# A graph-convolution kernel: 86 of 1592 row gathers replaced by column copies out of a feature table held in SBUF

## The chip, the cores and the metric

One Trainium2 chip, one core. The time is device time of that core in microseconds (us), from start to end of one execution; lower is better. Engines are named as in the profile: PE (TensorE), PEld (its weight loads), DVE (VectorE), ACT (ScalarE), POOL (GpSimd), SP (SyncE, which here only issues DMAs). A "q" behind an engine's name means its sequencer: instructions that are handled before the engine itself, such as register loads or DMA issues.

## The reference, cut to what matters

Two message-passing layers over a graph of 6250 nodes and 206,250 edges sorted by destination, 128 features. The change lies in the second:

```
edge_index = jnp.stack([src, dst])
...
h = jnp.maximum(_layernorm(x, axis=-1), 0.0)
...
filters = jax.nn.silu(edge_attr @ fW1 + fb1) @ fW2 + fb2
messages = (x[src] @ dW + db) * filters
aggregated = jax.ops.segment_sum(messages, dst, num_segments=x.shape[0])
upd = jax.nn.silu(aggregated @ uW1 + ub1) @ uW2 + ub2
return x + upd
```

Here `x[src]` is the normalised row `h` of each edge's source. The kernel computes `h @ dW + db` once per node, so an edge needs one row of a table of 6250 rows.

## The kernel before, in words

Edges are cut into **units** of 768: 6 chunks of 128 edges, one edge to a partition. 269 units make 45 **turns** of 6 units (the last has 5); the unit's place in its turn is its slot s. Because edges are sorted by destination, each unit adds into a window of 32 destination columns.

The program has three parts one after another: `prepare` (about 90 us: first layer norm, tables, windows), `attention_edges` (about 2000 us) and `convolution_edges` (about 2000 us). Attention gathers rows of 132 floats from table0; while it runs it finishes nodes in tiles of 128: normalises them, turns the tile with PE (features onto partitions), multiplies by dW, adds db and has SP store the rows to table1 in DRAM (L799) and the skip rows to `sent` (L800). The last seven tiles are done after the loop and stored at L814.

Convolution, for every unit n:

- **POOL** (`gather_units`, L688) issues one indirect DMA for each chunk (L63), which fetches 128 rows of 128 floats from table1 into `xg[:, s, c]`. It waits only for indices and for the slot to be free, that is for the message of the unit six before (L697, `xg_free` is `s_msg`). Each slot has its own arrival semaphore; `landed_by` (L556) gives its count. In every second turn one chunk of slot 4 is left out by POOL.
- **SP** (`load_indices`, L620; `Carry.collect`, L608) fetches that chunk in POOL's place with 128 DMAs of one row each, over two turns. It reads 16 row addresses at a time into registers (L613), issues 16 DMAs (L617), and copies the chunk into xg when the slot is free (L642).
- **ACT** computes SiLU of the hidden layer (L1387) and issues the loads of edge attributes (L1370).
- **PE** computes in iteration n the hidden layer of unit n (L1441), the filters of unit n-1 (L1417, needs the SiLU of n-1 and the message of n-3), and the sum over edges of unit n-3 (L1426). It also updates finished tiles (L1438, L1415).
- **DVE** adds in iteration n the sum of unit n-4 to the window (`merge`, L1504), makes the one-hot matrix of unit n-1 (L1484), adds the bias to its filters (L1490), waits for the gathered rows and multiplies (L1496). At the head of each turn it loads six window starts into registers (`bases`, L500).

The loops of DVE, ACT and PE have one turn as their body, written out unit by unit; POOL and SP have two and four. The addresses of gathered rows, windows and one-hot keys are registers; every instruction with such an address has a register instruction before it. `sums` is three planes of 6304 columns in SBUF: during convolution, plane 0 holds the sums and plane 1 the skip rows; plane 2 is free.

Of the kernel before, what the change touches and what calls it, by code (L numbers as in the profile page):

```python
# [24 lines left out]
P = 128  # L25
CH = 6
UE = CH * P
SL = 6
# [87 lines left out]
def prepare(nc, h, a, acc, state, typ, table, project, sources):  # L116


    with ExitStack() as ctx:
# [15 lines left out]
        dev, inv, shift, eps, early = sb("dev", [P, G]), sb("inv", [P, G]), sb("shift", [P, G]), sb("eps", [P, 1]), sb("early", [P, 1])  # L135
        ps_e, ps_x, ps_s, ps_l, ps_t = pb("ps_e"), pb("ps_x"), pb("ps_s", 512), pb("ps_l", 1024), pb("ps_t", 512)
# [17 lines left out]
        def _(sp):  # L154
# [28 lines left out]
            sp.dma_start(row_starts(state), a["src_rows"][:, :]).then_inc(lists_in, 16)  # L183
            project.load_rows(sp, a)
            for g in range(GROUPS - 1):
# [9 lines left out]
                if g:  # L195
                    store(g - 1)
            store(GROUPS - 2)
# [9 lines left out]
            sp.wait_ge(out_done[1], 16 * GROUPS)  # L207

        @block.gpsimd
        def _(pool):  # L210
# [44 lines left out]
            pool.wait_ge(lists_in, 16)  # L255
# [241 lines left out]

def bases(nc, engine, h, first, count):
# [40 lines left out]

LOAD = 3  # L540
# [15 lines left out]
def landed_by(pace, r, i, s, carried=0, j=0):  # L556

    if s != CARRY_SLOT:
# [61 lines left out]
def load_indices(nc, sp, a, h, idx, idx_in, gathered, landed, carry, xg, xg_free, ahead=lambda r, i, v: None, beside=lambda r, i: None,  # L620
                 behind=lambda r, i: None, listed=lambda: None):
# [22 lines left out]
    def span(r, t, b, first=False):  # L644

        for q in range(span_turns * LOADS):
# [4 lines left out]
            if q == 0 and first:  # L651
                listed()
# [35 lines left out]
def gather_units(pool, passes, table, xg, width, idx, idx_in, gathered, xg_free, pool_turn, carry):  # L688
    span_turns, carried_chunks = carry.pace.span, carry.pace.carried

    with pool.Fori(0, passes) as r:
        def turn(i, first, count, carried=None):
            for s in range(count):
# [5 lines left out]
                taken = carried is not None and s == CARRY_SLOT  # L699
# [21 lines left out]
def attention_edges(nc, h, a, acc, state, typ, table, messages, sent, y, project, sources, following):  # L721

    with ExitStack() as ctx:
# [23 lines left out]
        landed, pool_turn, steps, key_ready, begun, rise_zero = (  # L747
            sem(k) for k in "landed pool_turn steps key_ready begun rise_zero".split())
# [32 lines left out]
        def _(sp):  # L781
# [21 lines left out]
            sp.sem_inc(stored, 32)  # L803
            load_indices(nc, sp, a, h, idx, idx_in, gathered, landed, carry, xg, s_sum, beside=beside, behind=behind)
# [4 lines left out]
            sp.wait_ge(stored, 32 * (passes * DONE + 1))  # L809
            first_indices(sp, a, following.idx, following.idx_in)  # L810
            for n, k in enumerate((1, 0)):
                a0, a1 = HALVES[k]
                sp.wait_ge(t_hdc, n + 1)
                sp.dma_start(messages[(LAST + a0) * P:(LAST + a1) * P, :].rearrange("(t p) r -> p t r", p=P), l_hd[:, a0:a1, :]).then_inc(last_stored, 16)  # L814
            sp.wait_ge(last_stored, 32)

        @block.gpsimd
        def _(pool):
            gather_units(pool, project.pool_passes, table, xg, ROW, idx, idx_in, gathered, s_sum, pool_turn, carry)
# [18 lines left out]
        def _(act):  # L838
            nc.scalar.copy(acc[:, 1:NT, 0:NP], acc[:, 0, 0:NP].unsqueeze(1).to_broadcast([P, NT - 1, NP]))
            with act.Fori(0, pass_count(act, h)) as r:  # L840
# [55 lines left out]
                def relus(k):  # L896

                    act.wait_ge(stored, 32 * k)
# [162 lines left out]
        def _(dve):  # L1061
# [9 lines left out]
            with dve.Fori(0, pass_count(dve, h)) as r:  # L1071
                def tile(i, s):
# [4 lines left out]
                    if closes(i) and s == 1:  # L1077
                        dve.wait_ge(stored, 32 * (r * DONE + i - OPEN))
                        nc.vector.tensor_copy(p.turned, ps_c[:, P:2 * P])
                        nc.vector.tensor_tensor(p.relu, p.rows, p.relu, ALU.add)  # L1080
                    if closes(i) and s == 2:
                        nc.vector.tensor_tensor(p.turned, ps_c[:, 2 * P:3 * P], p.db, ALU.add)
# [180 lines left out]
class Project:  # L1263


    def __init__(self, nc, ctx):
        sb = lambda name, shape: ctx.enter_context(nc.sbuf_tensor("pj_" + name, shape, fp32))
        self.w, self.dw, self.bias = sb("w", [P, NT, D]), sb("dw", [P, D]), sb("bias", [P, NT, D])
        parts = sb("parts", [P, 3, D])
        self.relu, self.turned, self.db = (parts[:, k, :] for k in range(3))  # L1270
# [4 lines left out]
        self.carry_turn = ctx.enter_context(nc.semaphore("pj_carry_turn"))  # L1275
        self.raise_from = self.tile[:, :, 0:TILES]
# [23 lines left out]
def convolution_edges(nc, h, a, acc, update, table, sent, sources, project, y, out):  # L1300

    with ExitStack() as ctx:  # L1302
# [17 lines left out]
        sem_landed = sem("landed")  # L1320
# [304 lines left out]
```

## Time and profile before

| | us |
|---|---|
| median of 3 runs | 4103.61 (4102.91 to 4105.91) |
| span of the profiled execution (first to last instruction) | 4098.5 |
| mean granted TensorE clock in that execution | 0.60 |
| POOL busy | 3050.9 (74%) |
| PE busy | 3358.1 (82%) |
| DVE busy | 2405.1 (59%) |
| ACT busy | 1368.9 (33%) |

The runs give a time alone; the profile gives one further execution's span. Around its span lie launch and end, which no row divides. Busy shares are averages over three parts with different loads: DVE's, for example, is far higher in attention than in convolution. A matmul's end is modelled, and a POOL gather's busy time leaves out the sequencer's part between two of them.

### The profile page before, as it was taken

Reading aid. Unit: us, or ns where it says so; the run is one execution under the profiler, and the core shown is the slowest. Engines: PE = TensorE matmul, PEld = TensorE weight load, DVE = VectorE, ACT = ScalarE, POOL = GpSimd, SP = SyncE. Lnnn points to the kernel's source line nnn. Section 1 sums busy time; section 2 is a strip of 40 time slices with the busy share of each in tenths; the row PEclk is TensorE's granted clock in tenths of the full one; section 3 lists DMA queues with packets and bytes.
Section 4 is the critical chain, followed back from the end, with each engine's and each line's share of the span. In section 5 each row is a group of like instructions: output and inputs, shape, how many; then the busy total and the mean of one; then the engine's idle time right before and its main releaser. Section 6 shows DMA issues by size and latency. Waiting matters only on the chain. (4 is left out here: it accounts for less than half of the span.)

```text
span 4098.5 us, 63699 instructions
## 1 busy us (share of the span) xinstructions
PE 3358.1 (82%) x14005; PEld 2625.3 (64%) x14006; DVE 2405.1 (59%) x5327; ACT 1368.9 (33%) x3398; POOL 3050.9 (74%) x3216
## 2 busy tenths in 40 slices
PE   5788888888888888888768898888888888888798
PEld 3566666666666666666656676766766666666676
DVE  7888888888888888888853333333333332333333
ACT  5455555555555555555421111111111111111111
POOL 6777777777777777777757777777777777777776
PEclk7555555555555555555567666667666677667767
DMA  4222222222222222222232222222222222222222
GB/s 125 58 60 61 61 60 61 62 60 61 61 60 61 61 61 60 61 61 59 59 88 78 79 74 78 79 74 78 75 77 78 75 78 78 74 79 74 78 78 62
DMA packets 190049, 288.10 MB, mean 70 GB/s; under 512 B 85904, under 2 KB 132811, under 8 KB 185384
## 3 DMA queue, kind: packets, MB, share of 16 engines
q0 software_dynamic: 101888, 212.13, 20.6%
q1 hardware_dynamic: 83160, 33.99, 3.5%
q10 hardware_dynamic: 4840, 40.55, 3.2%
q14 instruction: 147, 1.20, 0.1%
q8 instruction: 14, 0.23, 0.0%
HBM read 271.07 MB, written 12.49 MB: 69 GB/s over the span
## 5 line engine op out<-in xcount | busy, mean ns | idle before, releaser
L63 POOL DMA_INDIRECT ce_xg<-table,ce_idx x1592 | 1509.2, 948 | 491.6 <-issue 481.5
L63 POOL DMA_INDIRECT ae_xg<-table,ae_idx x1592 | 1502.5, 944 | 491.2 <-issue 489.6
L1496 DVE TENSOR_TENSOR ce_msg<-ce_ring,ce_xg 128x768 f32<-128x768 f32 x269 | 257.6, 958 | 1151.0 <-DMA ce_xg<-table,ce_idx 1150.6
L948 PE MATMUL ae_ps_k<-ae_xg,ae_e 128*96 128x129 f32 x3224 | 882.7, 432 | 0.0
L1417 PEld LDWEIGHTS ce_ring<-ce_fw,ce_hid 128*128 128x128 f32 x3228 | 586.6, 278 | 435.6 <-DVE ce_msg L1496 314.6
L1417 PE MATMUL ce_ring<-ce_fw,ce_hid 128*128 128x128 f32 x3228 | 649.6, 377 | 262.1 <-DVE ce_msg L1496 261.8
L948 PEld LDWEIGHTS ae_ps_k<-ae_xg,ae_e 128*96 128x96 f32 x3224 | 689.6, 277 | 126.7 <-issue 117.2
L1387 ACT ACTIVATE ce_hid<-ce_ps_h,ce_fb 128x768 f32<-128x768 f32 x269 | 241.8, 899 | 1235.4 <-PE ce_ps_h L1441 692.2
L1441 PE MATMUL ce_ps_h<-ce_ea,ce_fw 50*128 50x384 f32 x1076 | 548.3, 641 | 19.0 <-DMA ce_ea<-in_edge_attr 17.1
L1426 PEld LDWEIGHTS ce_ring<-ce_hot,ce_msg 128*128 128x128 f32 x3224 | 528.4, 253 | 3.0 <-DVE ce_msg L1496 2.9
L1426 PE MATMUL ce_ring<-ce_hot,ce_msg 128*128 128x32 f32 x3224 | 514.3, 319 | 1.0 <-DVE sums L1504 1.0
L868 ACT ACTIVATE ae_off<-cst,plan 128x96 bf16<-128x96 f32 x1614 | 454.1, 363 | 5.0 <-DVE plan L491 5.0
L860 ACT ACTIVATE ae_upper<-ring 128x576 f32<-128x576 f32 x269 | 174.9, 650 | 668.3 <-DVE ring L1125 668.3
L996 PE MATMUL ring<-ae_rise,cst 64*128 64x192 f32 x538 | 270.4, 605 | 84.2 <-DVE ae_rise L1148 81.2
L963 PE MATMUL ae_ps_tz<-cst,ae_high 128*96 128x128 f32 x269 | 120.7, 449 | 251.8 <-DVE ae_high L1135 251.8
L1441 PEld LDWEIGHTS ce_ps_h<-ce_ea,ce_fw 50*128 50x128 f32 x1076 | 227.2, 234 | 145.1 <-issue 65.8
L1135 DVE TENSOR_REDUCE ae_high<-ae_e 128x96 f32<-128x576 f32 x269 | 304.8, 1133 | 0.0
L1490 DVE TENSOR_TENSOR ce_ring<-ce_ring,ce_fb 128x768 f32<-128x768 f32 x269 | 258.3, 960 | 71.5 <-PE ce_ring L1417 71.2
L1125 DVE TENSOR_TENSOR ring<-ring,ae_xg 128x576 f32<-128x576 f32 x269 | 206.1, 766 | 126.0 <-DMA ae_xg<-table,ae_idx 122.3
L963 PEld LDWEIGHTS ae_ps_tz<-cst,ae_high 128*96 128x96 f32 x269 | 41.9, 156 | 316.6 <-DVE ae_high L1135 316.6
L996 PEld LDWEIGHTS ring<-ae_rise,cst 64*128 64x128 f32 x538 | 134.0, 308 | 171.4 <-DVE ae_rise L1148 158.2
L844 ACT ACTIVATE ae_e<-ae_e 128x576 f32<-128x576 f32 x269 | 183.7, 683 | 105.6 <-DVE ae_e L1157 105.5
(186 smaller groups left out, 3336.2 us busy)
## 6 DMA issues: line engine op xcount, KB each, us to landing
ae_stage<-table SPq DMA_DIRECT2D x2560, 0.5 KB
ce_stage<-table SPq DMA_DIRECT2D x2560, 0.5 KB
ce_ea<-in_edge_attr ACTq DMA_DIRECT2D x88, 450.0 KB
ae_xg<-table,ae_idx POOLq DMA_INDIRECT x1592, 2.5
ce_xg<-table,ce_idx POOLq DMA_INDIRECT x1592
sums<-in_x SPq DMA_DIRECT2D x7, 448.0 KB, 4.6
table<-sums SPq DMA_DIRECT2D x6, 462.0 KB, 3.5
pj_bias<-in_x_rows SPq DMA_DIRECT2D x42, 64.0 KB
```

The source lines that it names most:

```text
L63: eng.indirect_dma_start(out=out, out_offset=None, in_=table[:, :], in_offset=bass.IndirectOffsetOnAxis(ap=idx, axis=0)).then_inc(done, 16)
L868: last = nc.scalar.activation(off[:, s % 2, c, :], h.iota, ACT.Square, bias=keys[:, c:c + 1], scale=STEP)
L948: last = nc.tensor.matmul(ps_k[0:KEYS, 0:D + 1], by_chunk[s % 3][:, c, :], xg[:, s % XS, c, 0:D + 1], start=(c == 0), stop=(c == count - 1))
L996: nc.tensor.matmul(ps_m[s % 2][:, 0:2 * KEYS], h.raised_by[0:64, :], rise[:, :, :].rearrange("p a k -> p (a k)"), start=True, stop=True).t ...
L1125: nc.vector.tensor_tensor(by_kind, by_kind, xg[:, s % XS, :, D + 1:ROW].unsqueeze(3).to_broadcast([P, CH, NT, W]), ALU.add).then_inc(s_ful ...
L1135: nc.vector.tensor_reduce(out=high[:, :], in_=by_chunk[s % 3].rearrange("p c k -> p k c"), op=ALU.max, axis=AX.X).then_inc(s_high, 1)
L1387: nc.scalar.activation(hid[:, b, :].rearrange("p (k e) -> p k e", k=2), ps_h[:, :].rearrange("p (k e) -> p k e", k=2)[:, :, 0:H], ACT.Silu ...
L1417: last = nc.tensor.matmul(ps_f[b][:, c * D:(c + 1) * D], hid[:, b, c * P:(c + 1) * P], fw2[:, :], start=True, stop=True)
L1426: last = nc.tensor.matmul(ps_a[s % 2][:, 0:W], msg[:, s % 3, c, :], hot[:, s % 3, c, :], start=(c == 0), stop=(c == count - 1))
L1441: last = nc.tensor.matmul(ps_h[:, k * 512:k * 512 + H], fw1[:, :], ea[:, s // LOAD, q:q + H], start=True, stop=True)
L1490: nc.vector.tensor_tensor(filt, filt, fb2[:, :].unsqueeze(1).to_broadcast([P, CH, D]), ALU.add).then_inc(s_bias, 1)
L1496: nc.vector.tensor_tensor(msg[:, s % 3, :, :], filt, xg[:, s % XS, :, :], ALU.mult).then_inc(s_msg, 1)
```

## The change

In each of the turns 2 to 44 (43 turns), the last chunk of slots 1 and 3 is no longer gathered by POOL. In its place:

- Attention stores the turned tile too, so that DRAM holds `features` [128 features][6272 nodes]: one more store by SP in each of 42 tiles and one for the last seven. The projected rows get a buffer of their own (`p.message`), so that the turned ones last until stored.
- `prepare` converts the 86 lists of 128 source nodes from 4-byte to 2-byte numbers on POOL and writes them to DRAM; convolution loads them into partition 0.
- Early in convolution SP loads all of `features` (128 partitions x 25,088 bytes) into plane 2 of `sums`.
- In turns 1 to 43, for two columns of work m = 0, 1 in slots 0-2 and 3-5: DVE copies nodes 0-63 and ACT nodes 64-127 of the list, each copy one column [128 x 1] from the table into `held`, at an address from a register. Registers are loaded eight at a time from 2-byte numbers. Batches are 24, 24 and 16 copies. ACT does this behind the unit's SiLU, DVE between the bias and the wait for the gathered rows.
- PE multiplies `held` by dW into 128 spare columns of a filter bank, ahead of the filters; DVE adds db and writes the chunk into xg (`place`). The chunk for slot 1 of the next turn is placed at slot 5, that for slot 3 at slot 2 of the next turn.
- Two semaphores become common to both layers (`pool_turn`, `carry_turn`), which changes no order.

```
+COLUMNS = (Column((0, 1, 2), 5, 1), Column((3, 4, 5), 2, 3))
+COLUMN_TURNS = TURNS - 2
+BATCHES = ((0, 24), (24, 48), (48, 64))
+ENGINE_SHARE = P // 2
+FETCH = 8
...
+def sources_at(nc, engine, columns, i, m, first):
+    return nc.values_load_multi_w_load_instructions(columns[:, bass.ds(((i - 1) * len(COLUMNS) + m) * P + first, FETCH)], engines=[engine],
...
-                taken = carried is not None and s == CARRY_SLOT
+                taken = carried is not None and s == CARRY_SLOT or s in to and not (isinstance(i, int) and i < 2)
                 for c in range(CH - 1 if taken else chunks_of(i, s)):
...
# attention_edges, SP, closes(i)
-                    sp.dma_start(messages[bass.ds((i - OPEN - 1) * P, P), :], p.turned).then_inc(stored, 16)
+                    sp.dma_start(messages[bass.ds((i - OPEN - 1) * P, P), :], p.message).then_inc(stored, 16)
+                    sp.dma_start(features[:, bass.ds((i - OPEN - 1) * P, P)], p.turned).then_inc(stored, 16)
...
# convolution_edges, SP, once, behind the first index load
+            def tables(r):
+                sp.wait_ge(scaled, 1)
+                sp.wait_ge(project.last_turned, 16)
+                sp.wait_ge(s_column, r * COLUMN_TURNS * len(COLUMNS) + len(COLUMNS))
+                sp.dma_start(by_node, features[:, :]).then_inc(table_in, 16)
...
# convolution_edges, ACT, behind the SiLU of slot s (DVE's is the same with columns e and tensor_copy, s_half)
+                def collect(i, s):
+                    m = s // 3
+                    e0, e1 = BATCHES[s % 3]
+                    if s % 3 == 0:
+                        act.wait_ge(s_column, column_at(r, i, m) + 1)
+                        act.sem_inc(begun, 1)
+                    if s == 0:
+                        act.wait_ge(table_in, 16 * (r + 2))
+                        act.sem_inc(begun, 1)
+                    for e in range(e0, e1, FETCH):
+                        nodes = sources_at(nc, mybir.EngineType.Activation, columns, i, m, ENGINE_SHARE + e)
+                        for k, node in enumerate(nodes, ENGINE_SHARE + e):
+                            last = nc.scalar.copy(held[:, m, k:k + 1], by_node[:, bass.ds(node, 1)])
+                    if s % 3 == 2:
+                        last.then_inc(s_other, 1)
...
# convolution_edges, PE, ahead of the filters of slot b
+                def products(i, m, b):
+                    k = column_at(r, i, m)
+                    pe.wait_ge(s_half, k + 1)
+                    pe.wait_ge(s_other, k + 1)
+                    nc.tensor.matmul(ps_x[b], held[:, m, :], project.dw[:, :], start=True, stop=True).then_inc(s_column, 1)
...
# convolution_edges, DVE
+                def place(i, m, b):
+                    column = COLUMNS[m]
+                    dve.wait_ge(s_column, column_at(r, i, m) + 1 + len(COLUMNS))
+                    dve.wait_ge(s_msg, r * UNITS + i * SL + column.to + 1 + XS)
+                    nc.vector.tensor_tensor(xg[:, column.to, CH - 1, :], ps_x[b], project.db, ALU.add).then_inc(s_placed, 1)
...
+                    aside(r, at)     # place, then collect
                     dve.wait_ge(s_bias, n)
                     carry.landed(dve, r, s, carried)
+                    for m, to in enumerate(TO):
+                        if s == to and not (isinstance(i, int) and i < 2):
+                            dve.wait_ge(s_placed, column_at(r, i - 1, m) + 2)
```

## Rows read from the trace of the kernel before

**Rows 1.** The chain that ended last, from the page:
```profile
POOL 35%; issue 12%; DMA 1%; POOLq 1%; DVE 0%; PE 0%; ACT 0%; DVEq 0%
```

**Rows 2.** Groups by line over the span: xcount | busy us, mean ns | idle us before
```profile
L63 POOL DMA_INDIRECT ce_xg<-table,ce_idx x1592 | 1509.2, 948 | 491.6 <-issue 481.5
L63 POOL DMA_INDIRECT ae_xg<-table,ae_idx x1592 | 1502.5, 944 | 491.2 <-issue 489.6
```

**Rows 3.** Gathers of POOL in order of time, the first and the last: start us, us
```profile
2091.94 0.98 POOL L63 DMA_INDIRECT ce_xg<-table,ce_idx  x1 [6.47 <-DVEq L1473]
...
4085.35 0.94 POOL L63 DMA_INDIRECT ce_xg<-table,ce_idx  x1 [0.30 <-issue]
```

**Rows 4.** Who waited for whom, 2200 to 4000 us: us in total, times, longest
```profile
DVE ce_msg L1496 <- DMA ce_xg<-table,ce_idx: 1057.0, 242, 10.3
...
POOL ce_xg L63 <- DVE ce_msg L1496: 3.3, 11, 0.3
```

**Rows 5.** Busy us of each engine in a stretch about one turn long
```profile
core 0: us, PE busy (x) PEld busy (x) DVE busy (x) ACT busy (x) POOL busy (x), PEclk, DMA share, GB/s
...
2545.00:2590.00 45.00, 34.36 (x178) 27.98 (x177) 14.07 (x27) 5.66 (x7) 34.03 (x37) 0.73 0.28 76
```

**Rows 6.** DVE: two one-column instructions in order of time; L1146, ns min/median/max
```profile
47.00 0.15 DVE L438 TENSOR_SCALAR narrow<-wide 128x1 f32<-128x1 f32 x1
47.07 0.14 DVE L439 TENSOR_SCALAR passes<-wide 128x1 int32<-128x1 f32 x1
...
L1146 DVEq FUSED_REGOPS  x269: 57/57/71, 84.4 to 2058.2; - x135
L1146 DVE COPY ae_rise<-state x269: 240/241/243, 85.2 to 2058.5; 1x96 f32 x135
```

**Rows 7.** ACT: one column, ns; six of L868 in order of time; L868, ns
```profile
L894 ACT ACTIVATE pj_few<-pj_few x42: 202/203/203, 202.8 to 2021.9; 128x1 f32<-128x1 f32 x42
...
2017.27 1.69 ACT L868 ACTIVATE ae_off<-cst,plan 128x96 bf16<-128x96 f32 x6
...
L868 ACT ACTIVATE ae_off<-cst,plan x1614: 358/362/374, 77.4 to 2041.0; 128x96 bf16<-128x96 f32 x180
L868 ACTq FUSED_REGOPS  x1476: 46/46/60, 205.1 to 2017.3; - x185
```

**Rows 8.** Register loads, ns: attention's eight values, convolution's six twice, SP's sixteen, one
```profile
L500 DVEq TENSOR_LOAD <-base_i x45: 752/1845/1868, 112.0 to 2055.9; - x45
...
L500 DVEq TENSOR_LOAD <-base_i x1: 1412/1412/1412, 3023.7 to 3023.7; - x1
...
L500 DVEq TENSOR_LOAD <-base_i x1: 805/805/805, 3068.4 to 3068.4; - x1
...
L613 SPq TENSOR_LOAD <-ce_lists x160: 1132/1208/1696, 2126.1 to 3881.8; - x160
...
L113 ACTq TENSOR_LOAD <-passes x2: 295/948/1600, 60.5 to 2097.4; - x2
```

**Rows 9.** SP's sequencer at its loop's end: last branch and what came next
```profile
L666 SPq COMPARE_BRANCH  x1: 61/61/61, 2467.6 to 2467.6; - x1
L666 SPq FUSED_REGOPS  x1: 154/154/154, 2470.4 to 2470.4; - x1
```

**Rows 10.** Two stretches of 10 us at either clock, columns as in rows 5
```profile
2142.00:2152.00 10.00, 8.37 (x56) 6.58 (x55) 2.20 (x4) 2.63 (x3) 7.56 (x9) 0.99 0.78 191
...
2182.00:2192.00 10.00, 10.00 (x33) 7.44 (x32) 2.29 (x4) 1.16 (x2) 7.55 (x9) 0.50 0.20 54
```

**Rows 11.** SP's issues in order of time: a tile's store, and three loads of 448 KB
```profile
2052.49 0.43 SPq L800 DMA_DIRECT2D sent<-pj_parts  x1
...
2124.39 1.68 SPq L1354 DMA_DIRECT2D sums<-sent  x3
```

**Rows 12.** DVE and POOL at convolution's start, in order of time
```profile
2092.42 5.31 DVE L1475 MEMSET sums<- 128x6304 f32 x1 [1.29 <-issue]
...
2095.73 4.15 POOL L63 DMA_INDIRECT ce_xg<-table,ce_idx  x1 [0.30 <-issue]
```

More of the change, by code:

```diff
@@ L537, in __init__, with collects, places, column_chunks @@
         self.chunks = (span * SL * np.arange(1, carried + 1) + CARRY_SLOT) * CH + CH - 1
+class Column:
+    def __init__(self, collected, placed, to):
+        self.collected, self.placed, self.to = collected, placed, to
+        self.late = placed < collected[-1]
+COLUMNS = (Column((0, 1, 2), 5, 1), Column((3, 4, 5), 2, 3))
+COLUMN_TURNS = TURNS - 2
+TO = [column.to for column in COLUMNS]
+BATCHES = ((0, 24), (24, 48), (48, 64))
+ENGINE_SHARE = P // 2
+FETCH = 8
+STORES = 48
+def collects(i):
+    return not (isinstance(i, int) and not 1 <= i <= COLUMN_TURNS)
+def places(i, column):
+    first = 2 if column.late else 1
+    return not (isinstance(i, int) and not first <= i < first + COLUMN_TURNS)
+def column_chunks():
+    turn = np.arange(2, TURNS)
+    return np.stack([(turn * SL + to) * CH + CH - 1 for to in TO], 1).reshape(-1)
+def column_at(r, i, m):
+    return r * COLUMN_TURNS * len(COLUMNS) + (i - 1) * len(COLUMNS) + m
 LOAD = 3
@@ L718, with attention_edges @@
 assert XS == SL
-def attention_edges(nc, h, a, acc, state, typ, table, messages, sent, y, project, sources, following):
+def attention_edges(nc, h, a, acc, state, typ, table, messages, features, sent, y, project, sources, following):
     with ExitStack() as ctx:
@@ L1268, in __init__ @@
         self.w, self.dw, self.bias = sb("w", [P, NT, D]), sb("dw", [P, D]), sb("bias", [P, NT, D])
-        parts = sb("parts", [P, 3, D])
-        self.relu, self.turned, self.db = (parts[:, k, :] for k in range(3))
+        parts = sb("parts", [P, 4, D])
+        self.relu, self.turned, self.db, self.message = (parts[:, k, :] for k in range(4))
         self.rows, self.x = (self.bias[:, k, :] for k in (1, 2))
@@ L1297, with convolution_edges @@
 UPDATE_SLOT = 3
-def convolution_edges(nc, h, a, acc, update, table, sent, sources, project, y, out):
+def convolution_edges(nc, h, a, acc, update, table, features, listed, by_node, sent, sources, project, y, out):
     with ExitStack() as ctx:
@@ L1415, in filters @@
                         nc.tensor.matmul(tile_y, one_hid[:, :], update.w2[:, :], start=True, stop=True).then_inc(t_v, 1)
+                    for m, column in enumerate(COLUMNS):
+                        if at is not None and at[1] == column.placed and places(at[0], column):
+                            products(at[0] - 1 if column.late else at[0], m, b)
                     for c in range(CH):
@@ L1443, in turn @@
                         if not (first and s < 1):
-                            filters(n - 1, (s - 1) % SL, first and s < 3, i if s else None)
+                            filters(n - 1, (s - 1) % SL, first and s < 3, i if s else None, (i, s))
                         if not (first and s < 3):
@@ L1485, in one_hot, with collect, aside, messages @@
                                             keys.unsqueeze(2).to_broadcast([P, CH, W]), ALU.is_equal)
-                def messages(n, s, i, carried, j=0):
+                def collect(i, s):
+                    m = s // 3
+                    e0, e1 = BATCHES[s % 3]
+                    if s % 3 == 0:
+                        dve.wait_ge(s_column, column_at(r, i, m) + 1)
+                        dve.sem_inc(begun, 1)
+                    if s == 0:
+                        dve.wait_ge(table_in, 16 * (r + 2))
+                        dve.sem_inc(begun, 1)
+                    for e in range(e0, e1, FETCH):
+                        nodes = sources_at(nc, mybir.EngineType.DVE, columns, i, m, e)
+                        for k, node in enumerate(nodes, e):
+                            last = nc.vector.tensor_copy(held[:, m, k:k + 1], by_node[:, bass.ds(node, 1)])
+                    if s % 3 == 2:
+                        last.then_inc(s_half, 1)
+                def place(i, m, b):
[3 more added lines that the diff above has]
+                    nc.vector.tensor_tensor(xg[:, column.to, CH - 1, :], ps_x[b], project.db, ALU.add).then_inc(s_placed, 1)
+                def aside(r, at):
+                    if at is None:
+                        return
+                    i, s = at
+                    for m, column in enumerate(COLUMNS):
+                        if s == column.placed and places(i, column):
+                            place(i - 1 if column.late else i, m, (s - 1) % SL % 2)
+                    if collects(i):
+                        collect(i, s)
+                def messages(n, s, i, carried, j=0, at=None):
                     filt = ps_f[s % 2][:, 0:CH * D].rearrange("p (c f) -> p c f", c=CH)
```

79 lines of the change are left out of this document (52 added, 27 removed).

## The prediction

> **What bounds the kernel now.** I read the chain of waits first: it names POOL and its issue, and nothing else above 1% [rows 1]. The groups by line say with what: 1592 gathers in convolution, 0.948 us busy each, and 0.3 us of issue between two [rows 2]. From the first to the last of them pass 1993.4 us [rows 3], 1.25 us a gather. Does POOL wait for anyone? The table of waits says no: in 1800 us it waited 3.3 us for DVE's messages, and nearly all its idle time is its own issue [rows 2]. The engine behind it, DVE, waits 1057 us for gathered rows [rows 4]. So convolution is 1592 x 1.25 us of POOL's work, with a short tail, and removing a gather removes 1.25 us, as long as what takes its place fits beside it. Attention is bound in the same way and keeps all its gathers.
>
> A turn has 36 chunks, less one in every second turn: 44.3 us. In it DVE is busy 14.1 us and ACT 5.7 us [rows 5]. The change spends that idle time.
>
> **What goes.** 2 x 43 = 86 gathers x 1.25 us = 107.5 us. A turn of POOL falls from 44.3 to 41.8 us. That is the most there is to gain.
>
> **What comes on DVE, per turn.** 128 copies of one column. Two static one-column instructions start 0.07 us apart though each lasts 0.15 us [rows 6]; an address from a register adds a register instruction of 0.057 us ahead [rows 6]. Sum 0.13 us, so 16.6 us. The bounds are 0.07 us (register step hidden) and 0.24 us (as long as the 96-column copy, no overlap [rows 6]): 9 to 31 us. I take 0.13, the sum of the rows nearest in shape.
>
> 16 register loads. No row loads 2-byte numbers. Nearest rows [rows 8]: eight 4-byte values 1.85 us; six 1.41 us in one turn and 0.81 us in the next; sixteen 1.13 to 1.21 us; one value 0.30 us at best. One account fits all: a value read alone costs about 0.24 us, and a 16-byte piece that starts on a multiple of 16 bytes costs about the same as a value. The six start at byte 24i - 16: a multiple of 16 only in even turns, where they are one piece and two values (3 x 0.27); else six (6 x 0.235). The eight start at 24i - 12, never a multiple: 8 x 0.23. The sixteen are four pieces: 4 x 0.28. The new lists hold eight 2-byte numbers, 16 bytes, on a multiple of 16. If the piece is counted in bytes, a load is one read, 0.3 to 0.5 us; if 2-byte numbers are read one by one, it is 1.85 us. I take 0.4 us (6.4 us a turn), because four reads are saved in every row where alignment allows it; the other end is the main rival.
>
> Here a page of the Trainium skill speaks against the change: "Runtime: NRT & Kernel Launch", Instruction fetch mechanics, gives about 200 ns for each register loaded, even in bulk. By it the loads would be 16 x 8 x 0.2 = 25.6 us a turn on each engine. By that rule, eight values at 1.85 us agree and sixteen at 1.21 us (0.075 each) do not [rows 8].
>
> The loop's body grows from some 60 to over 300 instructions. SP's body is of that size, and behind its last branch 2.8 us pass before the next instruction [rows 9]. I charge DVE and ACT 2.8 us a turn; bounds 0 and twice that, if two blocks are fetched.
>
> Two placements per turn: 0.3 us each, somewhat over the 96-column copy [rows 6]. DVE's sum: 14.1 + 16.6 + 6.4 + 1.1 (window starts, mean of the two in rows 8) + 0.6 + 2.8 = 41.6 us if nothing overlaps, against POOL's 41.8. But most of the loads overlap: the sequencer reads registers while the engine works off the 2.3 us (a sixth of 14.1 [rows 5]) of message, merge, one-hot and bias that each unit queues ahead. Up to 2 us a unit are hidden this way, so about 35 us. It fits, with 7 us to spare.
>
> **On ACT**: six L868 take 1.69 us at 0.362 us each, so they start 0.265 us apart, overlapping by 0.10 [rows 7]. A one-column instruction of 0.203 us [rows 7] then starts every 0.105 us; with its register step of 0.046 us 0.12, at most 0.25 us. 128 x 0.12 = 15.4 us, loads 6.4, own work 5.7, branch 2.8: 30 us of 41.8. Behind the collect of a unit (24 x 0.12 + 3 x 0.4 = 4.1 us) waits ACT's next SiLU, and PE waits for that. PE's iteration is 28 matmul records: at the low clock (granted 0.50, 1.2 GHz) 33 run in 10 us, so 8.5 us; at the high one (0.99, 2.4 GHz) 56 in 8.4 us, so 4.2 us [rows 10]. SiLU (0.9 us, a sixth of 5.66 [rows 5]) + 4.1 us fit inside 8.5 but not inside 4.2, so PE catches up at 5 to 5.5 us a unit in place of 4.2. POOL now asks for a unit every 7.0 us. Two products a turn add 2 of 28 records twice, 1.2 us at the low clock. PE works at either clock by turns; it still catches up.
>
> **Ring.** DVE's wait on a product or on the table holds the merges and messages queued behind it, and POOL's gather waits for the message of six units before: 6 x 7.0 less landing, some 35 us of slack. POOL waits at 3.3 us in 1800 today, so this slack is nearly unused [rows 4].
>
> **Opening.** SP issues the 3.2 MB table behind three loads of 448 KB at about 2126 us [rows 11]. DMA moved 191 GB/s in a stretch with such a load against 54 GB/s without [rows 10], so some 140 GB/s are free: 4.5 MB land by about 2158. DVE and ACT want it near 2143 (36 gathers after 2092, the 3 us that one of them lost [rows 12], landing), so they stand some 15 us, covered by the 35. Cost 0; bound 10 us. The next four `sent` loads and 128 staged rows queue behind the table on SP's ring; they are due at turn 2, after 2180.
>
> **Small parts, SP's queue.** 42 more stores by SP at 0.43 us [rows 11], one of last tiles, one list store and two list loads: SP's attention stores lie where POOL waits for nobody; at the change of stages about 1 us shows. `prepare` adds a small POOL conversion. Together 2 us, bounds 0 and 6.
>
> **Sum.** The profiled execution spans 4098.5 us, 5.1 below the median of 4103.6, which holds launch and end too. 4098.5 - 107.5 + 4 (2 of small parts, 2 of waits by bunching) = 3995 span; by the median 4000 us. This case's own range is 3993 to 4022.
>
> **Rivals.**
> *A, DVE is full (slower).* Place: the register loads in DVE's `collect`. At 1.85 us each, 16 are 29.6 us; 35.2 + 29.6 less 12 hidden (2 us in each of six units) is 53 us a turn, against 44.3 before: 43 x 8.7 = +374, 4478 us. The point from which it decides: full gain up to 1.15 us a load, nothing left from 1.3 us. For it: eight values do cost 1.85 today, and no row has 2-byte numbers. Against: aligned rows are cheap. ACT would be full at the same time.
> *B, part of the gain.* Loads near 1.2 us, copies near 0.2 us, or PE late at the low clock: 4022 to 4095 us.
> *C, copies hold POOL off.* 3.8 DVE copies fall on each gather. A gather beside a DVE memset took 4.15 us [rows 12]. If each copy kept POOL off for 0.1 us, a gather would come every 1.63 us and a turn take 33.5 x 1.63 = 54.6 us, 4547 in all; at 0.03 us, 45.7 us, 4164. Against: gathers in attention, beside 96-column copies, are as short (0.944 us) as in convolution [rows 2, 6]. For this rule see "SBUF — State Buffer", Who interferes with whom: an fp32 copy in a two-port mode locks GpSimd out of a shared port. [...]
> *D, PE.* Waits for late SiLUs break up its work, the granted clock stays at 0.50, and 8.5 us plus 0.2 us of products a unit exceed POOL's 7.4 of before: 52 us a turn, 4440; half of that if only at times. Against: ACT's 5 us fit inside the low clock's 8.5.
> *E, it does nothing.* The gathers left out could be hidden anyway; rows 4 exclude that.
>
> **Chances.** Forecast 0.62; B 0.10; a result within 0.2% (8 us; about what a measurement of this kernel can tell from no change) 0.03; A 0.16; C 0.05; D 0.04. Faster: 0.72; slower 0.25. The overall range is 3993 to 4280: it takes in B and the milder half of C and D.
>
> **What would show it.** Right: 1506 gathers in convolution, still 0.95 us each and 1.25 apart; POOL's wait for L1496's successor still a few us; new DVE and ACT copy groups of 5504, starting 0.13 and 0.12 us apart; register loads of 0.3 to 0.5 us; DVE still waiting for gathered rows in most units. Wrong: loads over 1.2 us, POOL waiting for messages, DVE's waits for DMA gone (A); gathers longer than 1 us (C); granted clock near 0.5 with PE busy all through convolution (D).

## The result, and the profile after

| | before | after |
|---|---|---|
| median of 4 runs, us | 4104.76 (4102.91 to 4105.97) | 4761.07 (4757.27 to 4763.82) |
| span of the profiled execution | 4098.5 | 4760.1 |
| mean granted TensorE clock | 0.60 | 0.56 |

The change costs 656 us: ratio 1.160, 95% interval 1.158 to 1.161. The forecast was 4000 us, the range 3993 to 4280. What happened is rival A, DVE full by its register loads, and its price of 4478 was itself some 280 us short. DVE's turn, from branch to branch of its loop, takes 60.5 us on average; POOL's was 44.4 before.

The chain of the kernel after, by engine and by line, stands against [rows 1], where POOL held 35%:

```profile
DVEq 25%; DVE 16%; issue 13%; PE 1%; DMA 1%; POOL 0%; SPq 0%; ACT 0%; POOLq 0%
DVEq L506 22%; DVE ce_held L1599 10%; DVE ce_ring L1624 3%; DVE ce_hot L1583 1%; DVEq L512 1%; DVEq L1599 1%; DMA sums<-features 0%; DVE ce_msg L1634 0%; DVE sums L1642 0%; POOL ce_xg L63 0%; DVE ce_xg L1608 0%; DVEq L1583 0%; DVEq L1642 0%
```

POOL is gone from the chain. A quarter of the span is DVE's sequencer (DVEq), and nearly all of that is one line: L506, the register loads of the node lists, 22%. Second come the copies (L1599).

Next the groups by line: count, busy us and mean ns, idle before. They answer to [rows 2].

```profile
L63 POOL DMA_INDIRECT ce_xg<-table,ce_idx x1506 | 1425.1, 946 | 1214.2 <-DVE ce_msg L1634 793.9
L63 POOL DMA_INDIRECT ae_xg<-table,ae_idx x1592 | 1502.9, 944 | 491.2 <-issue 487.5
L1599 DVE COPY ce_held<-sums 128x1 f32 x5504 | 716.1, 154 | 1080.0 <-issue 1079.6
L1473 ACT COPY ce_held<-sums 128x1 f32 x5504 | 624.2, 191 | 1058.9 <-issue 1058.4
```

The 86 gathers are gone, and those left are as short as before (0.946 us), also beside 5504 DVE copies. But POOL, which waited 3.3 us for DVE's messages in 1800 [rows 4], now waits 794 us for them. The group of the copies shows where DVE's time is: it stood idle 1080 us ahead of them with the label "issue": it waited for nothing that the profile shows, and its own sequencer was at work.

The table of waits between 2300 and 4600 us (us in total, times, longest) has no line for DVE waiting for gathered rows, which led it before with 1057 us [rows 4]:

```profile
DVE ce_held L1599 <- issue: 964.5, 720, 2.3
ACT ce_held L1473 <- issue: 926.2, 611, 1.8
POOL ce_xg L63 <- DVE ce_msg L1634: 747.9, 191, 8.8
...
PE ce_ring L1508 <- DVE ce_msg L1634: 249.2, 90, 5.8
```

So the order of who waits for whom has turned round: PE and POOL wait for DVE, DVE and ACT mostly for their own sequencers. The line that had to be bounded blind, register loads of 2-byte numbers (ns min/median/max):

```profile
L506 ACTq TENSOR_LOAD <-ce_columns x688: 1707/1723/1964, 2149.2 to 4704.1; - x172
L506 DVEq TENSOR_LOAD <-ce_columns x688: 1822/1826/1937, 2149.2 to 4715.2; - x172
```

Eight 2-byte numbers take DVE 1.83 us, 0.228 us each, though all of them lie in one aligned 16-byte piece. That is the dear end of the bound (1.85), to 0.02 us.

What one such load does is to be seen in DVE's timeline (start, us, what, idle before):

```profile
3000.76 0.96 DVE L1634 TENSOR_TENSOR ce_msg<-ce_ring,ce_xg 128x768 f32<-128x768 f32 x1
3001.64 0.18 DVE L1642 TENSOR_TENSOR sums<-sums,ce_ring 128x32 f32 x1
3001.73 0.35 DVE L1583 TENSOR_TENSOR ce_hot<-cst,key 128x192 f32<-128x192 f32 x1
3002.00 0.95 DVE L1624 TENSOR_TENSOR ce_ring<-ce_ring,ce_fb 128x768 f32<-128x768 f32 x1
3003.53 1.04 DVE L1599 COPY ce_held<-sums 128x1 f32 x8 [0.57 <-issue]
3006.49 1.04 DVE L1599 COPY ce_held<-sums 128x1 f32 x8 [1.92 <-issue]
```

A message, a merge, a one-hot and a bias are queued; beside them the first load runs, and only some 0.5 us of it show (the gap is 0.57). Eight copies follow in 1.04 us (0.126 us from start to start), and the next load stands alone: 1.92 us of an idle engine. Three such groups make a unit's collect.

### The profile page after: what moved, and what is told of

It is laid out like the page before. It is cut to its first block, busy times and chain, and to the rows that moved or that the text cites. A ratio compares the mean times of both kernels' runs of the same rounds, so it can differ in the third digit from the quotient of the medians.

```text
span 4760.1 us, 89708 instructions
## 1 busy us (share of the span) xinstructions
PE 3620.1 (76%) x14177; PEld 2847.9 (60%) x14178; DVE 3125.0 (66%) x10917; ACT 1993.6 (42%) x8903; POOL 2967.4 (62%) x3131
## 4 chain that ended last, share of the span: by engine, by line
DVEq 25%; DVE 16%; issue 13%; PE 1%; DMA 1%; POOL 0%; SPq 0%; ACT 0%; POOLq 0%
DVEq L506 22%; DVE ce_held L1599 10%; DVE ce_ring L1624 3%; DVE ce_hot L1583 1%; DVEq L512 1%; DVEq L1599 1%; DMA sums<-features 0%; DVE ce_msg L1634 0%; DVE sums L1642 0%; POOL ce_xg L63 0%; DVE ce_xg L1608 0%; DVEq L1583 0%; DVEq L1642 0%; DVEq L627 0%; DVEq L1633 0%
## 5 line engine op out<-in xcount | busy, mean ns | idle before, releaser
L63 POOL DMA_INDIRECT ce_xg<-table,ce_idx x1506 | 1425.1, 946 | 1214.2 <-DVE ce_msg L1634 793.9
L1599 DVE COPY ce_held<-sums 128x1 f32 x5504 | 716.1, 154 | 1080.0 <-issue 1079.6
L1473 ACT COPY ce_held<-sums 128x1 f32 x5504 | 624.2, 191 | 1058.9 <-issue 1058.4
L1508 PE MATMUL ce_ring<-ce_fw,ce_hid 128*128 128x128 f32 x3228 | 751.6, 422 | 288.0 <-DVE ce_msg L1634 288.0
L1508 PEld LDWEIGHTS ce_ring<-ce_fw,ce_hid 128*128 128x128 f32 x3228 | 702.3, 326 | 410.2 <-DVE ce_msg L1634 372.5
L1539 PE MATMUL ce_ps_h<-ce_ea,ce_fw 50*128 50x384 f32 x1076 | 598.1, 692 | 25.7 <-DMA ce_ea<-in_edge_attr 16.6
L1517 PEld LDWEIGHTS ce_ring<-ce_hot,ce_msg 128*128 128x128 f32 x3224 | 584.4, 276 | 19.2 <-DVE sums L1642 18.2
L1517 PE MATMUL ce_ring<-ce_hot,ce_msg 128*128 128x32 f32 x3224 | 567.2, 339 | 14.4 <-DVE sums L1642 14.4
L1525 PE MATMUL ce_ring<-pj_dw,ce_held 128*128 128x128 f32 x172 | 65.7, 485 | 372.8 <-DVE ce_msg L1634 357.7
L1525 PEld LDWEIGHTS ce_ring<-pj_dw,ce_held 128*128 128x128 f32 x172 | 42.9, 309 | 439.8 <-issue 439.8
```

The costliest lines, as they stand in the source:

```text
L63: eng.indirect_dma_start(out=out, out_offset=None, in_=table[:, :], in_offset=bass.IndirectOffsetOnAxis(ap=idx, axis=0)).then_inc(done, 16)
L1473: last = nc.scalar.copy(held[:, m, k:k + 1], by_node[:, bass.ds(node, 1)])
L1508: last = nc.tensor.matmul(ps_f[b][:, c * D:(c + 1) * D], hid[:, b, c * P:(c + 1) * P], fw2[:, :], start=True, stop=True)
L1517: last = nc.tensor.matmul(ps_a[s % 2][:, 0:W], msg[:, s % 3, c, :], hot[:, s % 3, c, :], start=(c == 0), stop=(c == count - 1))
L1539: last = nc.tensor.matmul(ps_h[:, k * 512:k * 512 + H], fw1[:, :], ea[:, s // LOAD, q:q + H], start=True, stop=True)
L1599: last = nc.vector.tensor_copy(held[:, m, k:k + 1], by_node[:, bass.ds(node, 1)])
```

## The experiments

Theory 1 is the reading so far: 2-byte numbers are read one by one, and these loads fill DVE's sequencer. Two others were put to the test: that the copies and the longer loop body fill DVE whatever a load costs (theory 2), and that POOL or PE at its low clock sets the turn once gathers are taken away (theory 3). Each line that begins with "-" is one of the changed kernel. Every batch had runs of the kernel before beside it; beside the first four kernels below it took 4105.3 us (7 runs).

**Lists of 4-byte numbers, on a multiple of 16 bytes.** The lists come straight from the 4-byte input, DVE's halves on partition 0 and ACT's on partition 1; copies, loop bodies and all else stay:

```
-        columns = sb("columns", [1, COLUMN_TURNS * len(COLUMNS) * P], u16)
+        columns = sb("columns", [2, COLUMN_TURNS * len(COLUMNS) * ENGINE_SHARE], i32)
...
-    ... columns[:, bass.ds(((i - 1) * len(COLUMNS) + m) * P + first, FETCH)]
+    ... columns[first // ENGINE_SHARE:first // ENGINE_SHARE + 1,
+                bass.ds(((i - 1) * len(COLUMNS) + m) * ENGINE_SHARE + first % ENGINE_SHARE, FETCH)]
```

> The lists are kept as 4-byte numbers, 64 of each engine's half on a partition of its own, so that each read of eight starts on 16 bytes. Theory 1 (the changed kernel is held by VectorE's sequencer, which reads the 2-byte numbers one by one, 16 reads of 1.83 us a turn): a read takes 0.5 to 0.65 us, the turn loses 16 x 1.2 = 19 us and falls to POOL's 41 to 43 us, the time to 4000 to 4060 us. Theory 2 (the copies and the longer loop body hold VectorE, whatever the reads cost): 4500 us or more. Theory 3 (POOL or TensorE at its low clock sets the turn once gathers go on chip): 4400 us or more, with POOL or PE ahead in the chain.

Measured: 3995.89 us, ratio 0.974 (0.972 to 0.975). Its loads, its chain, and its waits between 2300 and 4000 us:

```profile
L506 ACTq TENSOR_LOAD <-ce_columns x688: 537/550/772, 2146.3 to 3933.8; - x172
L506 DVEq TENSOR_LOAD <-ce_columns x688: 592/599/686, 2147.2 to 3941.4; - x172
```
```profile
POOL 27%; issue 12%; DVE 3%; DVEq 2%; PE 2%; DMA 1%; POOLq 1%; ACT 0%
```
```profile
DVE ce_held L1599 <- issue: 306.8, 542, 1.1
...
DVE ce_msg L1634 <- DMA ce_xg<-table,ce_idx: 39.5, 26, 5.4
...
POOL ce_xg L63 <- DVE ce_msg L1634: 3.4, 11, 0.3
```

A load takes DVE 0.60 us, a third of before. So the tile does start on a multiple of 16 bytes; the 2-byte one stands behind the same tiles in the code. POOL is back in the chain, and its wait for messages back at 3.4 us. With the same copies and the same loop body the change gives its full gain, 109 us, so theories 2 and 3 fall. This version beats both kernels here (not in the slower batches below). It has little left, though: DVE waited for rows for 39.5 us in 1700, and for PE 23, together 1.5 us a turn, where the kernel before waited for rows 1057 us in 1800. DVE's turn, from branch to branch of its loop, is 41.9 us on average, POOL's pace.

**The same lists, one number further on.** Same 4-byte numbers, in a tile one number longer and filled from its second number, so that no load starts on a multiple of 16 bytes:

```
-                bass.ds(((i - 1) * len(COLUMNS) + m) * ENGINE_SHARE + first % ENGINE_SHARE, FETCH)]
+                bass.ds(1 + ((i - 1) * len(COLUMNS) + m) * ENGINE_SHARE + first % ENGINE_SHARE, FETCH)]
```

> As the lists of 4-byte numbers, but with the whole list one number further on, so that no read of eight starts on 16 bytes. If the price goes by aligned pieces of 16 bytes (each read is then 3 numbers, one whole piece, 1 number, or all one by one): a read takes 1.2 to 1.9 us and the time is 4400 to 4760. If only the size of the numbers counts: a read stays at 0.5 to 0.65 us and the time at that of the aligned lists.

Measured: 4776.97 us, ratio 1.163 (1.161 to 1.165), and the loads:

```profile
L506 ACTq TENSOR_LOAD <-ce_columns x688: 1735/1757/1992, 2144.9 to 4717.4; - x172
L506 DVEq TENSOR_LOAD <-ce_columns x688: 1841/1846/1977, 2146.5 to 4730.7; - x172
```

Four bytes of offset cost 781 us. This pair is the cleanest of the experiments, since the two kernels have the same instructions and differ in the address alone. It is also not "three single, one piece, one single", which would be five reads: at 1.85 us all eight are read singly. So whether a load goes by pieces hangs on where it starts and how wide its numbers are: 4-byte numbers from an aligned start do, 2-byte ones from an aligned start don't. Starts of 2-byte lists off a multiple of 16 were not run.

**Two loads a turn in place of 16, 2-byte lists**, on both engines:

```
+                        if e == 0:
+                            dve_nodes[m] = sources_at(nc, mybir.EngineType.DVE, columns, i, m, e)
+                        nodes = dve_nodes[m]          # ACT's likewise
-                        nodes = sources_at(nc, mybir.EngineType.DVE, columns, i, m, e)
```

> 2-byte lists as in the change, but each engine reads its lists twice a turn instead of 16 times and takes the same eight nodes for all 64 copies of a column (the columns so gathered are not the ones the computation asks for; the count of copies is the same). Theory 1: 14 reads of 1.83 us less on each engine, the turn at POOL's pace, 4000 to 4060 us. Theory 2: still 4500 or more. Theory 3: still 4400 or more.

Measured: 3998.27 us, ratio 0.974 (0.972 to 0.976). The loads that are left still take 1.83 us each; DVE waits for gathered rows again, 476.8 us in 1700:

```profile
L506 DVEq TENSOR_LOAD <-ce_columns x86: 1824/1834/1955, 2147.3 to 3922.5; - x86
```
```profile
DVE ce_msg L1642 <- DMA ce_xg<-table,ce_idx: 476.8, 149, 8.5
```

With DVE far from full the time is not shorter than with the 4-byte lists: 3996 to 3998 us is POOL's floor. This experiment alone would not single out the loads, since it also takes away register instructions and shortens the loop's body (see "Half the loads" below); the 4-byte pair does.

**Two loads a turn on ACT alone.**

> Only ScalarE reads its lists twice a turn; VectorE reads them 16 times as in the change (ScalarE's half of the columns are not the ones asked for). Theory 1 with VectorE as the one that sets the turn: 4740 to 4765 us, nothing changed. If the two engines' reads hold each other up or ScalarE sets part of the turn: 4300 to 4700.

Measured: 4764.28 us, ratio 1.160 (1.159 to 1.162): the changed kernel's time, as theory 1 has it. DVE alone sets it.

**Two loads a turn on DVE alone.** (The kernel before, beside this one and the next: 4102.89 us.)

> Only VectorE reads its lists twice a turn; ScalarE reads them 16 times as in the change (VectorE's half of the columns are not the ones asked for). Theory 1: VectorE's turn falls to some 34 us. ScalarE's sum: 16 x 1.72 + 128 x 0.101 + six SiLUs of 0.9 + issues of loads = 27.5 + 12.9 + 5.4 + 1.5 = 47 to 49 us, above POOL's 41.8, so the time is 4761 - 43 x 12 = 4250, 4200 to 4300 us, ScalarE ahead in the chain. If ScalarE's reads are hidden under its waits: 4000.

Measured: 4245.03 us, ratio 1.035 (1.033 to 1.037), as forecast. Its chain by engine and by line:

```profile
ACTq 31%; issue 8%; ACT 8%; PE 2%; DMA 1%; POOL 0%; SPq 0%; DVE 0%; POOLq 0%; DVEq 0%
ACTq L506 27%; ACT ce_held L1473 8%; ACTq L1438 3%; ACTq L1473 1%; ACT ce_hid L1455 1%; PE ce_ring L1508 1%; PE ce_ps_h L1539 0%; PE ce_ring L1517 0%; DMA sums<-features 0%; POOL ce_xg L63 0%; ACTq L1448 0%; DMA ce_xg<-table,ce_idx 0%; ACTq L530 0%; PE ce_ps_h L1549 0%; ACT ce_one_hid L1454 0%
```

ACT was the second engine too full, at 47.7 us a turn, hidden behind DVE's 60.5. Moving work from DVE to ACT could not have saved the 2-byte lists: half of 47.7 + 60.5 is 54 us, over the 44.4 of before.

**Half the loads, 2-byte lists**: as above with `if e % 16 == 0`, on both engines.

> 2-byte lists, each engine reads 8 times a turn instead of 16 and uses each read's eight nodes for 16 copies (half the columns are not the ones asked for). Theory 1 (VectorE's turn is a plain sum of reads, copies, refetch and its own work, 60.5 us in the change): 8 x 1.83 = 14.6 us less, 45.9 us a turn, and over 43 turns 4761 - 43 x 14.6 = 4133 us; 4030 to 4140 if the refetch behind the loop's branch (2.75 us) shrinks with the shorter body. If reads overlapped with other engines' work and only the last few counted: 4000, as with two reads a turn.

Measured: 3997.31 us, ratio 0.975 (0.973 to 0.976): a miss of theory 1 by 33 to 136 us, at the value named for the rival. The rows say why. DVE's copies and the register instructions ahead of them, and its loop branch with what follows, in this kernel:

```profile
L1607 DVE COPY ce_held<-sums x5504: 135/152/157, 2148.5 to 3942.2; 128x1 f32 x197
L1607 DVEq FUSED_REGOPS  x2752: 57/57/65, 2148.4 to 3941.6; - x197
```
```profile
L627 DVEq COMPARE_BRANCH  x2: 50/53/56, 2433.2 to 2433.4; - x2
L627 DVEq MOVE  x2: 36/40/43, 2433.6 to 2433.7; - x2
```

and in the changed kernel:

```profile
L1599 DVEq FUSED_REGOPS  x5504: 57/57/65, 2151.1 to 4718.0; - x197
```
```profile
L627 DVEq COMPARE_BRANCH  x2: 59/61/63, 2424.9 to 2425.1; - x2
L627 DVEq MOVE  x2: 48/48/49, 2427.9 to 2427.9; - x2
```

The experiment took away more than loads. The register instruction belongs to a value loaded, not to a copy: 5504 became 2752, and by the start times in order a copy that uses a value a second time starts 0.061 us after the last one in place of 0.126. That is 64 x 0.065 = 4.2 us a turn. And the pause behind the loop's branch went from 2.8 to 0.2 us. Together 60.5 - 14.6 - 4.2 - 2.6 = 39.1 us, under POOL's 41.8, so the floor. That the loads overlap with other work more than assumed is excluded, since their hidden part is the same as in the changed kernel (7.3 us a turn of 15.8, against 7.1 of 30.4).

The sum still is not the whole. Between 2600 and 4000 us (33.3 turns of 42.0 us) DVE waited in this kernel:

```profile
DVE ce_msg L1642 <- DMA ce_xg<-table,ce_idx: 146.5, 62, 5.4
...
DVE ce_ring L1632 <- PE ce_ring L1512: 49.9, 29, 3.7
...
DVE sums L1650 <- PE ce_ring L1521: 14.9, 12, 1.4
```

That is 6.3 us a turn, so its own turn is near 35.7 us and not 39.1. A part of the other 3.4 us is steps that go with each load (the gap ahead of eight copies is 1.92 us for a load of 1.83); the rest is not taken apart.

**Runs that tell little.** In three batches every kernel, the one before included, took about a third longer (before: 5436, 5486 and 5493 us), attention too, which the experiments don't touch. The texts below expect times at the usual pace, so no time among them can be compared as it stands. POOL's timeline in attention, from the first of these kernels, has 1.25 us from gather to gather and then a hole, without a gather being longer:

```profile
421.00 0.94 POOL L63 DMA_INDIRECT ae_xg<-table,ae_idx  x1 [0.30 <-issue]
422.25 0.94 POOL L63 DMA_INDIRECT ae_xg<-table,ae_idx  x1 [0.30 <-issue]
429.23 0.94 POOL L63 DMA_INDIRECT ae_xg<-table,ae_idx  x1 [6.03 <-PE ae_ps_k L1003]
```

What causes it I did not find. All kernels of these batches lie 3 to 6% above the kernel before, whatever was taken away, the aligned 4-byte lists too, which gained 2.6% above. So the batches don't rank the theories, the gain of the 4-byte lists is shown for the usual pace alone, and why it turns into a loss here stays open. Only durations of single instructions carry over.

First batch, the kernels with edits shown above (before: 5436 us):

4-byte lists:

> The lists are kept as 4-byte numbers, DVE's half on partition 0 and ACT's on partition 1, loaded from the input and not from the 2-byte copy; still eight values a load, now 32 bytes on a multiple of 32. Theory 1 (2-byte numbers are read one by one, and these loads fill DVE's sequencer): a load falls from 1.83 to about 0.55 us (two 16-byte pieces), DVE's turn from 60.5 to 60.5 - 16 x 1.28 = 40 us, under POOL's 41.8, so 4000 to 4020 us and POOL waits for nobody again. Theory 2 (the copies and the long loop body fill DVE, loads are a symptom or cost the same for any type): loads stay near 1.8 us and the time near 4760. Theory 3 (PE at the low clock, broken up by late SiLUs, sets the turn): loads may fall, but the time stays above 4500.

Measured: 5668 us, ratio 1.042 (1.038 to 1.046). Loads took 0.55 us on ACT and 0.60 on DVE, as theory 1 has it.

Two loads a turn on both engines:

> As changed, but each engine loads its eight registers once per column of work (2 loads a turn) and uses them for all 64 copies; the other nodes' values are left out, all copies and all else stay. Theory 1: DVE's turn 60.5 - 14 x 1.83 = 35 us, POOL bounds, about 4000 us. Theory 2 (copies and loop body): stays above 4500. Theory 3 (PE): above 4500.

Measured: 5619 us, one run.

Two loads a turn on DVE alone:

> As e2, but only DVE's loads are thinned; ACT keeps 16 of 1.72 us. Tells whether ACT alone would be full too: per turn 16 x 1.72 + 128 x 0.10 + 5.7 of its own = 46 us, some of it beside its SiLU. Theory 1 with ACT full second: a turn of 44 to 48 us, 4100 to 4300. If ACT has room: about 4000.

Measured: 5584 us, one run; the chain has ACT's loads at 19%.

Two loads a turn on ACT alone:

> As e2, but only ACT's loads are thinned; DVE keeps 16 of 1.83 us. Theory 1: DVE alone sets the turn, 4740 to 4765 as changed. Theory 3 (PE broken up by SiLUs that wait behind ACT's collect): well under 4700, since ACT's collect falls from some 8 to 3 us.

Measured: 5753 us, one run; the chain has DVE's loads at 18%. This one was the longest of the four, as theory 1 has it, but the kernel before it in this list was the shortest, and theory 1 puts it behind the first two: the order proves nothing.

Second and third batch, the same four kernels in each (before: 5486 and 5493 us). Half the loads:

> 2-byte lists, each engine reads 8 times a turn instead of 16 and uses each read's eight nodes for 16 copies (half the columns are not the ones asked for). Theory 1 (VectorE's turn is a plain sum of reads, copies, refetch and its own work, 60.5 us in the change): 8 x 1.83 = 14.6 us less, 45.9 us a turn, and over 43 turns 4761 - 43 x 14.6 = 4133 us; 4030 to 4140 if the refetch behind the loop's branch (2.75 us) shrinks with the shorter body. If reads overlapped with other engines' work and only the last few counted: 4000, as with two reads a turn.

> 2-byte lists, each engine reads 8 times a turn instead of 16 and uses each read's eight nodes for 16 copies (half the columns are not the ones asked for). Theory 1 (VectorE's turn is a plain sum of reads, copies, refetch and its own work, 60.5 us in the change): 8 x 1.83 = 14.6 us less, 45.9 us a turn, and over 43 turns 4761 - 43 x 14.6 = 4133 us; 4030 to 4140 if the refetch behind the loop's branch (2.75 us) shrinks with the shorter body. If reads overlapped with other engines' work and only the last few counted: 4000, as with two reads a turn.

Measured: 5700 and 5744 us, ratios 1.041 (1.038 to 1.044) and 1.045 (1.042 to 1.048).

One copy for each load, eight columns wide, in place of eight copies:

```
-                        for k, node in enumerate(nodes, e):
-                            last = nc.vector.tensor_copy(held[:, m, k:k + 1], by_node[:, bass.ds(node, 1)])
+                        last = nc.vector.tensor_copy(held[:, m, e:e + FETCH], by_node[:, bass.ds(nodes[0], 1)].to_broadcast([P, FETCH]))
```

> 2-byte lists, all 16 reads a turn on each engine, but one copy of a repeated column per read instead of eight (seven of eight columns are not the ones asked for). Theory 1: 112 copies less x 0.126 us = 14.1 us, the turn 46.4 us and 4155 us; if the refetch of 2.75 us goes too with the shorter body, 43.7 us and 4040 us. If the copies hid behind the reads: still about 4760. If the reads cost next to nothing without copies behind them: 4000.

> 2-byte lists, all 16 reads a turn on each engine, but one copy, of one repeated column, per read instead of eight (seven of eight columns are not the ones asked for). Theory 1: 112 copies less x 0.126 us = 14.1 us, the turn 46.4 us and 4155 us; if the refetch of 2.75 us goes too with the shorter body, 43.7 us and 4040 us. If the copies hid behind the reads: still about 4760. If the reads cost next to nothing without copies behind them: 4000.

Measured: 5626 and 5671 us, ratios 1.028 (1.023 to 1.034) and 1.036 (1.033 to 1.039). It decides nothing.

Two loads a turn on DVE alone:

> Only VectorE reads its lists twice a turn; ScalarE reads them 16 times as in the change (VectorE's half of the columns are not the ones asked for). Theory 1: VectorE's turn falls to some 34 us. ScalarE's sum: 16 x 1.72 + 128 x 0.101 + six SiLUs of 0.9 + issues of loads = 27.5 + 12.9 + 5.4 + 1.5 = 47 to 49 us, above POOL's 41.8, so the time is 4761 - 43 x 12 = 4250, 4200 to 4300 us, ScalarE ahead in the chain. If ScalarE's reads are hidden under its waits: 4000.

> Only VectorE reads its lists twice a turn; ScalarE reads them 16 times as in the change (VectorE's half of the columns are not the ones asked for). Theory 1: VectorE's turn falls to some 34 us. ScalarE's sum: 16 x 1.72 + 128 x 0.101 + six SiLUs of 0.9 + issues of loads = 27.5 + 12.9 + 5.4 + 1.5 = 47 to 49 us, above POOL's 41.8, so the time is 4761 - 43 x 12 = 4250, 4200 to 4300 us, ScalarE ahead in the chain. If ScalarE's reads are hidden under its waits: 4000.

Measured: 5675 and 5686 us, ratios 1.034 (1.030 to 1.039) and 1.035 (1.032 to 1.038).

4-byte lists, and sixteen copies a turn more:

```
+                            if e == 0:
+                                nc.vector.tensor_copy(again[:, m, k:k + 1], by_node[:, bass.ds(node, 1)])
```

> The aligned 4-byte lists, and VectorE repeats the first eight copies of each column into a spare tile: 16 copies, 2.0 us, more a turn. If VectorE's turn (9.6 of reads + 16.1 of copies + 2.7 of refetch + 13 of its own) stands right at POOL's 41.8 us, as its chain with only a few per cent says: 43.5 to 43.9 us a turn and 4060 to 4085 us. If POOL alone sets the turn with room on VectorE: 3996.

> The aligned 4-byte lists, and VectorE repeats the first eight copies of each column into a spare tile: 16 copies, 2.0 us, more a turn. If VectorE's turn (9.6 of reads + 16.1 of copies + 2.7 of refetch + 13 of its own) stands right at POOL's 41.8 us, as its chain with only a few per cent says: 43.5 to 43.9 us a turn and 4060 to 4085 us. If POOL alone sets the turn with room on VectorE: 3996.

Measured: 5640 and 5650 us, ratios 1.027 (1.025 to 1.030) and 1.030 (1.027 to 1.034). It decides nothing. How near DVE stands to the edge with the 4-byte lists thus rests on its waits and its turn alone, and the cost of the copies on the rows, not on a run at the usual pace that adds or takes away copies.

## Why the prediction was wrong

**The step that failed** is the price of a register load: "I take 0.4 us (6.4 us a turn)". It measured 1.83 us, 29.2 us a turn. The account behind it (a single value 0.24 us; an aligned 16-byte piece as much as one value) was right in all it was built on, and the 4-byte lists confirm it: two pieces, 2 x 0.27 = 0.54 us, measured 0.55 on ACT and 0.60 on DVE. What failed is the step from there to 2-byte numbers: every row of the account held 4-byte values, and I let "counted in bytes" decide, since alignment saved reads in every row (three reads for each piece of four values, not the four of the text). No row could tell 2-byte from 4-byte numbers, so 0.4 and 1.85 deserved nearer equal chances than 0.62 and 0.16; and with the break-even at 1.3 us the two ends were 480 us apart by my own sum.

The Trainium skill's rule in "Runtime: NRT & Kernel Launch", Instruction fetch mechanics (about 200 ns for each register, even in bulk), spoke against the change, and was set aside. The page tells it of loads from HBM; those here are from SBUF. By it an estimate of 16 x 8 x 0.2 = 25.6 us a turn stood against 29.2 measured on DVE: for the 2-byte numbers and the 4-byte ones off their start (0.215 to 0.231 us a value) it is up to 13% low. The aligned 4-byte loads, at 0.069 to 0.075 us a value, do not follow it.

**Of the rest of the sum, POOL's part and the copies held; what is hidden and the pause behind the branch did not.** With the load at 0.60 us the time is 3995.89 us, 4 from the forecast, but DVE came in under POOL by 1.5 us a turn and not by 7, so that this nearness says little of DVE's sum. Point by point:

- Gain of 107.5 us, less 4 for small parts and waits: the 4-byte lists gained 109.4. Each gather was worth its 1.25 us; the 4 us did not show.
- Copies 0.13 and 0.12 us apart: 0.126 and 0.101. Placements 0.3: 0.279. Opening: "some 15 us" of standing for the table from 2143 was right in size by luck. DVE stood 15.1 us, but from 2130.8 to 2145.9 and for gathered rows, while the table was under way; with the 4-byte lists it was 9.5 us, and POOL never waited there.
- Pause behind the branch, 2.8 us on both engines: on DVE 2.8, on ACT 0.2. ACT's loop holds some 320 instructions a turn, DVE's 370. DVE's with half the loads has some 290, and there the pause is gone. SP's body, from which the price was taken as "of that size", has 606 instructions, so that the match on DVE is in part luck.
- Hidden part of the loads, "up to 2 us a unit": the load in the timeline above had 1.4 us hidden, and over all records of 2600 to 3800 us 7.1 of 30.4 us of loads a turn lie over busy time of the engine, 1.2 us a unit. "7 us to spare" was thus wrong: with loads of 0.60 us DVE fits, with 1.5 us over.

**Rival A** named the mechanism, the place and the signs (loads over 1.2 us, POOL waiting for messages, DVE's waits for DMA gone; each came true). Its 53 us a turn became 60.5. Its 35.2 + 29.6 less the 7.1 really hidden is 57.7; the other 2.8 us are of the size of the sequencer's small steps (register instructions alone lie over 1.6 us a turn of DVE's idle time), which the sum left out. From the turn, 43 x (60.5 - 44.4) = 692 us; measured were 662 of span. The ring's slack of some 35 us, which the first turn uses up, is of the size of the difference; no run shows that.

**B** did not come: the load lay at its dear end, not between the ends. **C** falls: gathers stayed at 0.946 us and, with the 4-byte lists, 1.253 apart beside the same copies. **D** falls: the mean clock did drop to 0.56, but PE was busy for only 73% of 2300 to 4600 us and waited for DVE's messages; with 4-byte lists the clock is back at 0.60 and the time at 3996. "ACT would be full at the same time": nearly right, at 47.7 us a turn it is over the 44.4 of before (4245 us) but 13 us behind DVE.

## What to carry to other kernels

Before registers are loaded in bulk, fix two things about the list in memory: 4-byte numbers, and every load starting on a multiple of 16 bytes. On this kernel missing either one costs 765 us and more against the aligned 4-byte lists, and the sequencer's time is shown by no busy share: look for idle time labelled "issue" ahead of short instructions. When a term's two ends decide the sign and no row has the operation itself, the chance should sit near the middle, however well an account fits neighbouring rows; and when an experiment shares loaded values between instructions, count the register instructions and the loop's length that go with them.

## What the runs showed of the hardware that I had not expected

- A register load of eight 2-byte numbers from an aligned start takes as long as eight single values (0.228 us each on DVE, 0.215 on ACT); so does one of eight 4-byte numbers from a start 4 bytes off (1.85 us on DVE, against 0.60 from an aligned start).
- DVE pays the loads at 0.60 us where ACT pays 0.55, and 1.83 where ACT pays 1.72.
- The pause behind a loop's branch was 0.2 us in bodies of some 290 (DVE) and 320 instructions (ACT), and 2.8 us in one of some 370 (DVE), 2.5 to 2.8 in one of 606 (SP, kernel before). The matmul engine's body has some 370 to 385 instructions and no such pause. What decides it no run here shows.
- One-column copies whose address register is already made start 0.061 us apart on DVE, at 0.135 to 0.157 us each.
